# Two transformer blocks on one core: queue entries set behind their producers, staging by head groups, another opening order, and three PSUM banks for the last stage

## The reference

```
for layer in (0, 1):
    h = layernorm(x) * n1_g + n1_b
    x = attention(h, h,   q1, k1, v1, o1) + x      # 512 keys
    h = layernorm(x) * n2_g + n2_b
    x = attention(h, ctx, q2, k2, v2, o2) + x      # 1601 keys
    h = layernorm(x) * n3_g + n3_b
    a, g = split(h @ ff_w1 + ff_b1)
    x = (a * gelu(g)) @ ff_w2 + ff_b2 + x          # exact gelu
```

## Time and profile before

| | |
|---|---|
| median of 3 runs | 3865.36 us (3864.6 to 3879.61) |
| the profiled execution | 3857.31 us |
| its span | 3855.5 us |
| busy: PE, DVE, ACT, POOL | 3224.7, 2090.1, 1996.1, 624.3 us |
| mean granted clock of PE | 0.914 of full speed |

### The profile page before, as it was taken

The page is one execution under the profiler, slowest core; times in us unless marked ns, Lnnn a source line. Parts: engine busy times, 40 slices in busy tenths (PEclk is TensorE's granted clock), DMA queues, the critical chain, the costliest instruction groups (busy, mean ns, idle before and its releaser), DMA issues.

```text
span 3855.5 us, 43782 instructions
## 1 busy us (share of the span) xinstructions
PE 3224.7 (84%) x16320; PEld 1495.8 (39%) x16320; DVE 2090.1 (54%) x2565; ACT 1996.1 (52%) x3816; POOL 624.3 (16%) x676
## 2 busy tenths in 40 slices
PE   3686788899789878989889887898989979887867
PEld 1233343334344433534345332444334534533334
DVE  2554565667546655567546655555756645455410
ACT  1353366556555555556554565555655556454521
POOL 2113121212202121021201132021210031001010
PEclk9798898889899988999889998999989989998979
DMA  2642335431433344332333445333333133222202
GB/s 72 159 133 60 81 87 139 113 92 43 120 94 86 81 96 114 78 104 65 109 92 78 114 111 144 94 92 84 87 100 82 44 84 103 59 40 51 65 17 68
DMA packets 194323, 340.88 MB, mean 88 GB/s; under 512 B 19192, under 2 KB 101504, under 8 KB 192832
## 3 DMA queue, kind: packets, MB, share of 16 engines
q1 hardware_dynamic: 194112, 338.08, 33.7%
HBM read 202.29 MB, written 114.75 MB: 82 GB/s over the span
## 4 chain that ended last, share of the span: by engine, by line
PE 62%; DMA 11%; DVE 9%; ACT 6%; SPq 5%; issue 4%; POOL 3%; ACTq 0%; DVEq 0%; POOLq 0%
PE po L1053 12%; PE pr L1038 12%; PE pd L1019 8%; DVE mx L854 7%; DMA QS<-scr_q 6%; PE pf L969 5%; PE pf L977 5%; PE pf L916 4%; PE pf L957 3%; PE pf L939 3%; PE pf L948 3%; ACT ET L779 3%; DMA scr_k<-HS 2%; SPq L513 2%; PE pf L972 2%
## 5 line engine op out<-in xcount | busy, mean ns | idle before, releaser
L779 ACT ACTIVATE ET<-pr 128x512 f32<-128x512 f32 (+1 forms) x2720 | 1478.4, 597 | 1418.5 <-PE pr L1038 1406.0
L854 DVE TENSOR_REDUCE mx<-pd 128x2 f32<-128x804 f32 (+2 forms) x1600 | 1582.7, 1032 | 1056.2 <-PE pd L1019 1052.7
L1038 PE MATMUL pr<-QS,KS 64*128 64x512 f32 (+1 forms) x2720 | 877.1, 514 | 80.4 <-ACT ET L779 77.9
L1019 PE MATMUL pd<-KS,QS 64*128 64x400 f32 (+2 forms) x3200 | 636.4, 396 | 308.3 <-DMA QS<-scr_q 200.8
L1053 PE MATMUL po<-ET,V 128*32 128x512 f32 (+2 forms) x5440 | 779.9, 648 | 0.8 <-issue 0.6
L1038 PEld LDWEIGHTS pr<-QS,KS 64*128 64x128 f32 (+1 forms) x2720 | 345.3, 188 | 948.4 <-ACT ET L779 638.1
L1019 PEld LDWEIGHTS pd<-KS,QS 64*128 64x128 f32 x3200 | 374.4, 200 | 422.8 <-DMA QS<-scr_q 213.5
L673 POOL TENSOR_TENSOR HS<-uT,HS 128x512 fp32r<-128x512 f32 (+2 forms) x168 | 190.0, 1131 | 737.6 <-ACT uT L744 737.6
L969 PE MATMUL pf<-HS,WS 128*128 128x512 f32 x800 | 241.1, 433 | 72.2 <-DVE uT L847 24.9
L689 POOL TENSOR_TENSOR OA<-OA,DEN 128x512 f32<-128x512 f32 (+1 forms) x48 | 60.9, 1269 | 1311.4 <-DVE DEN L862 1311.4
L862 DVE RECIPROCAL DEN<-DEN 128x128 f32<-128x128 f32 (+1 forms) x192 | 170.5, 922 | 104.4 <-DMA DEN<-OU 103.7
(11 more groups left out here) (63 smaller groups left out, 2174.7 us busy)
## 6 DMA issues: line engine op xcount, KB each, us to landing
WS<-parts SPq DMA_DIRECT2D x160, 320.0 KB, 2.9
KS<-scr_k SPq DMA_DIRECT2D x80, 600.8 KB, 10.3
QS<-scr_q SPq DMA_DIRECT2D x80, 512.0 KB, 10.6
scr_k<-HS SPq DMA_DIRECT2D x144, 200.0 KB
scr_q<-HS SPq DMA_DIRECT2D x96, 256.0 KB
KS<-scr_k SPq DMA_DIRECT2D x80, 192.0 KB, 3.6
scr_k<-HS SPq DMA_DIRECT2D x48, 256.0 KB
OA<-OU SPq DMA_DIRECT2D x320, 32.0 KB
```

Source lines behind the costliest of these rows:

```text
L779: activation(ET[0:q.rows[k], s % 2, 2 * pair + e, :], pr[e][0:q.rows[k], :], ACT.Exp).then_inc(score_free, 1)
L854: v.reduce_max(mx[:, t, 2 * p:2 * p + 2, c], pd[no % 2][:, :, 0:cols], AX_X).then_inc(unit_free, 1)
L1019: ins = mm(pd[no % 2][:, e, 0:cols], queries[:, t * P:(t + 1) * P], keys, start=True, stop=True)
L1038: mm(pr[e][0:m, :], keys, queries, start=True, stop=True).then_inc(score_ready, 1)
```

## The change

- **SP's order.** `beside` becomes three functions: loads are queued `LOAD` = 2 beats behind their fill, stores 4 (`STORE`), bias rows 8 (`LOAD_ROW`). `MOVE` goes from 6 to 8, `INVERT` from (13, 15, 17, 19) to (14, 15, 16, 17), `DIVIDE` from 20 to 18.
- **Staging.** `KEY_JOBS` puts all key columns of a block of eight heads together; `split_for(q)` names the last fill that a group needs, and only that is waited for. Units start at `_at + 7`.
- **Prologue.** Of q1 and k1 only the first fill of each stands before the first beat; the others go into phase (None, 0). In phase (None, 1) v2a and a part of k2 come first, the rest of k2 and of q1, k1 of pass 2 goes to phase (0, 2). The memsets of KS come after the first statistics. v1 of pass 1 is set step by step into the last steps of phase (None, 0).
- **Bias rows** are added to X after the fourth normalisation, not after each.
- **Fills.** `deal_by_steps` gives each step one fill, or two of the short ones (t1, t2, t3, tc); ff2 has two parts of ten matmuls (`half`, `ff2`) at two steps; a gate starts with 4 fills of a instead of 3; two fills of v2a stand before t3. This holds for phases with a self and a cross pass, without those that split ff_w1 for `deal_by_steps`.
- **Last stage.** From `TAIL` (o2 of pass 7) fills go round `pf`, `pr[0]`, `pr[1]`, each with its own semaphore; g of pass 7 is evicted by Gelu itself; X of a layer 1 pass is stored tile by tile.

```diff
@@ -50,11 +50,15 @@
 V2B_GROUP = 2
+KEY_JOBS = [(c, n, cols) for c in range(KC) for n, cols in CHUNKS]
...
@@ -74,7 +78,8 @@
 def gate(i, together):
-    return [("gelu", i, 0)] + places("a", i, 0, together), places("a", i, together) + places("ff2", i)
+    return [("gelu", i, 0)] + places("a", i, 0, together), (
+        places("a", i, together) + [p for f in range(TT) for p in (("half", i, f), ("ff2", i, f))])
@@ -84,17 +89,25 @@
 def stages_beside(c, i):
     if c is None and i == 0:
-        seq = (mixed(places("tc", 0), places("n1", 1)) + places("t1", 1) + places("q1", 1) + places("k1", 1)
-               + places("k2", 0))
+        seq = [p for f in range(1, KC) for p in (("q1", 0, f), ("k1", 0, f))]
+        seq += mixed(places("tc", 0, 0, 3), places("n1", 1)) + places("t1", 1)
+        seq += [p for f in range(KC) for p in (("q1", 1, f), ("k1", 1, f))]
+        seq += places("tc", 0, 3) + places("k2", 0, 0, len(CHUNKS))
     elif c is None:
-        seq = (places("v1", 1) + places("o1", 0) + mixed(places("v2a", 0), places("n2", 0)) + places("t2", 0)
-               + mixed(places("q2", 0), places("n1", 2)) + places("t1", 2) + places("q1", 2) + places("k1", 2))
+        at = len(CHUNKS)
+        seq = places("v2a", 0) + [p for f in range(TT) for p in (("o1", 0, f), ("n2", 0, f))]
+        seq += places("k2", 0, at, at + 2) + places("t2", 0) + places("q2", 0, 0, 1)
+        seq += mixed(places("k2", 0, at + 2, 2 * at), places("n1", 2)) + places("q2", 0, 1) + places("t1", 2)
+        seq += [("q1", 2, 0), ("k1", 2, 0)]
     elif c == N - 1:
         first, rest = gate(c - 1, 3)
         seq = places("v2b", c) + mixed(places("o2", c - 1), []) + places("n3", c - 1) + places("t3", c - 1)
         seq += places("g", c - 1) + [first] + rest
     else:
         seq = places("v1", i) if i is not None else places("v2b", c)
+        if c == 0:
+            seq += [("q1", 2, 1), ("k1", 2, 1)] + places("k2", 0, 2 * len(CHUNKS))
+            seq += [("q1", 2, 2), ("k1", 2, 2)]
         seq += (places("o2", c - 1) if c else []) + places("o1", c + 1)
         cross = places("tc", c + 1)
         if i is not None:
...
@@ -105,10 +118,11 @@
         seq += places("k2", c + 1)
         if c % B == 0:
             seq = mixed(seq, places("w", c // B))
+        behind = places("v2a", c + 1)
         if c:
-            first, rest = gate(c - 1, 3)
-            seq += places("t3", c - 1) + places("g", c - 1) + [first] + rest
-        behind = places("v2a", c + 1)
+            first, rest = gate(c - 1, 4)
+            seq += behind[:2] + places("t3", c - 1) + places("g", c - 1) + [first] + rest
+            behind = behind[2:]
         if c + 3 < N:
             behind = mixed(behind[:2], places("n1", c + 3)) + behind[2:]
             behind += places("t1", c + 3) + places("q1", c + 3) + places("k1", c + 3)
...
@@ -116,7 +130,7 @@
     return [p if isinstance(p, list) else [p] for p in seq]
-BEFORE = places("n1", 0) + places("t1", 0) + places("q1", 0) + places("k1", 0) + places("v1", 0)
...
@@ -175,6 +189,13 @@
+COPY, MOVE, INVERT, DIVIDE = 5, 8, (14, 15, 16, 17), 18
+LOAD, STORE, LOAD_ROW = 2, 4, 8
...
+SHORT = ("t1", "t2", "t3", "tc")
+def deal_by_steps(stretches, steps):
+    slots, kinds = [], []
+    for stretch in stretches:
+        works = [p[0] for p in stretch if p[0] in STAGE or p[0] == "half"]
+        if works and works[0] in SHORT and slots and kinds[-1] == works[0] and len(slots[-1]) == 1:
+            slots[-1].append(stretch)
+        elif slots and kinds[-1] is None:
+            slots[-1][-1] = slots[-1][-1] + stretch
+            kinds[-1] = works[0] if works else None
+        else:
+            slots.append([stretch])
+            kinds.append(works[0] if works else None)
+    assert len(slots) <= len(steps)
+    for k, slot in enumerate(slots):
+        for n, stretch in enumerate(slot):
+            PLACES.setdefault(4 * steps[k * len(steps) // len(slots)] + 1 + 2 * n, []).extend(stretch)
...
+        for _f in range(TT):
+            PLACES.setdefault(4 * (_from - TT + _f + 1) + 5, []).append(("v1", _i, _f))
+        _v2a = len(VALUE_FILLS["v2a"])
+        deal(_all[:_v2a], _odd[2:2 + 2 * _v2a])
+        _q2 = [("q2", 0, 0)]
+        _fast = _all.index(_q2) + 1
+        _behind = [b for b in _odd if b > 4 * _from + DIVIDE]
+        _fills = sum(p[0] in STAGE for s in _all[_v2a:_fast] for p in s)
+        deal(_all[_v2a:_fast], _behind[:_fills])
+        deal(_all[_fast:], _behind[_fills:])
+    elif _i is not None and _c % B:
+        deal_by_steps(_all, range(_from + 1, _to))
     else:
         deal(_all, _odd[2::2])
 PLACES[BEATS + BEATS_BEHIND] = list(BEHIND)
...
+TAIL = FILL["o2", N - 1, 0]
+def split_for(q):
+    own = [("q" if x == "q" else "k") + ("1" if q.kind == "S" else "2") for x in "qk"]
+    fills = [(own[0], q.i, q.g // 2)]
+    if q.kind == "S":
+        fills.append((own[1], q.i, q.g // 2))
+    else:
+        fills.append((own[1], q.i, len(CHUNKS) * (q.g // 2 + 1) - 1))
+    return max(fills, key=lambda p: SPLIT[p])
...
-    _at = max(4 * _host.end if _host else FIRST_BEAT, _stored + 1 if _stored >= 0 else FIRST_BEAT)
+    _at = max(4 * _host.end if _host else FIRST_BEAT, _stored + STORE + 1 if _stored >= 0 else FIRST_BEAT)
     STAGE_AT.setdefault(_at, []).append(_q)
     if _q.n == 0:
         TURN_AT[FIRST_BEAT] = _q
         continue
-    _from = max(_at + 5, _free, 0)
+    _from = max(_at + 7, _free, 0)
...
-    _free = _beats[-1] + _lag + 1
+    _free = _beats[-1] + _lag + 2
...
-COPY, MOVE, INVERT, DIVIDE = 5, 6, (13, 15, 17, 19), 20
...
+        def free(no):
+            return fill_free if no < TAIL else tail_free[(no - TAIL) % len(tail_free)]
+        def freed_through(no):
+            if no < TAIL:
+                return [(fill_free, no + 1)]
+            return [(free(m), (m - TAIL) // len(tail_free) + 1) for m in range(max(no - len(tail_free) + 1, TAIL), no + 1)]
+        def bank(no):
+            return pf if no < TAIL else (pf, pr[0], pr[1])[(no - TAIL) % len(tail_free)]
...
+            for p in BEFORE:
+                stores_behind(*p)
+                loads_behind(*p)
+            for p in BEFORE:
+                row_behind(*p)
+            for beat in range(FIRST_BEAT, BEATS + BEATS_BEHIND + LOAD_ROW + 1):
+                for p in PLACES.get(beat - LOAD, []) if beat - LOAD >= 0 else []:
+                    loads_behind(*p)
+                for p in PLACES.get(beat - STORE, []) if beat - STORE >= 0 else []:
+                    stores_behind(*p)
+                for p in PLACES.get(beat - LOAD_ROW, []) if beat - LOAD_ROW >= 0 else []:
+                    row_behind(*p)
                 for q in STAGE_AT.get(beat, []):
...
-                pool.wait_ge(w_in["b"], LOADED["b", stage, i])
-                pool.wait_ge(norm_done, at + 1)
-                gp.tensor_tensor(X[:, b, t, :], X[:, b, t, :], brow[:, :], ALU.add).then_inc(bias_done, 1)
+                if t == TT - 1:
+                    pool.wait_ge(w_in["b"], LOADED["b", stage, i])
+                    pool.wait_ge(norm_done, at + 1)
+                    for k in range(TT):
+                        gp.tensor_tensor(X[:, b, k, :], X[:, b, k, :], brow[:, :], ALU.add).then_inc(bias_done, 1)
...
+                    activation(uT[:, f * T:(f + 1) * T], pf[:, :], ACT.Gelu if i == N - 1 else ACT.Identity,
+                               bias=b1col[:, l, 1, f:f + 1]).then_inc(done, 1)
...
+            def set_key_rows():
...
+                    set_key_rows()
...
+                if stage == "half":
+                    pe.wait_ge(fill_free, FILL["ff2", i, f])
+                    feed_back(bank(FILL["ff2", i, f]), i, f, range(FM // 2))
...
+                no, pf = FILL[stage, i, f], bank(FILL[stage, i, f])
+                if 0 < no <= TAIL:
+                    pe.wait_ge(fill_free, no)
+                elif no >= TAIL + len(tail_free):
+                    pe.wait_ge(free(no), (no - TAIL) // len(tail_free))
...
-                    if q.g == 0:
-                        pe.wait_ge(fill_free, filled("v1" if q.kind == "S" else "v2a", q.i))
+                    if q.g == 0 and q.kind == "C":
...
+                if q.g == 0 and q.kind == "S":
+                    pe.wait_ge(fill_free, FILL["v1", q.i, k] + 1)
...
```

More of the change, by code:

```diff
@@ L184, in deal @@
 def deal(stretches, beats):
-    count = sum(any(p[0] in STAGE for p in stretch) for stretch in stretches)
+    count = sum(any(p[0] in STAGE or p[0] == "half" for p in stretch) for stretch in stretches)
     k = 0
@@ L198 @@
     elif _c is None:
-        deal(_all[:TT], list(range(4 * _from + 4, 4 * _from + 8)))
-        deal(_all[TT:], [b for b in _odd if b > 4 * _from + 22])
+        for _f in range(TT):
[10 more added lines that the diff above has]
+        deal_by_steps(_all, range(_from + 1, _to))
     else:
@@ L413, in blocks_kernel @@
         fill_free = sem("fill_free")
+        tail_free = [sem(f"tail_free{i}") for i in range(3)]
         low_done = sem("low_done")
```

(9 more changed lines are left out.)

146 lines of the change are left out of this document (78 added, 68 removed).

## The result

The kernel after the change takes 3717.33 us (median of 4 runs, 3704.01 to 3730.65), the kernel before 3864.98 (4 runs). The ratio is 0.961, with a 95% interval of 0.9568 to 0.9652: 3.9% less time, where 6.7% was forecast (3608 us). The direction came as forecast and the two ends gave at least what was forecast; the middle gave back little more than a quarter of what was forecast there, and the time is by number that of case B (3718). The profiled execution took 3730.65 us, its span is 3728.8, its granted clock 0.925.

The account below looks back on a forecast made before the run. PE was taken to bound the middle, with its idle and lower-clock time to win. From the 3857.3 us execution, -50+11-9-150-70-12+40-17 = -257 gave 3600, so 3608 us for the median; range 3480 to 3765.

Parts of the forecast that it names:

- case B: Half of the middle's gain, waits moving to chunks, ACT holds for HS or DMA bandwidth: 3718 us (3690-3760), chance 0.22.
- Prologue, -50: Before the first unit: memsets 31.4 us, bias additions 2.6 and four projections 16.1 leave the path, together -50 us.
- the wait of 9.2 us in phase (None, 0): PE's wait at 132.9 for DVE, behind second-sequence statistics, goes as four projections come ahead: -9 us (0 to -9).
- contention at nothing: Prologue: DVE memsets beside POOL normalisations stop nothing, 0 us; a full block would be +31.
- Last stage, -17: Tail, 3711 us to the end: fills of g and save 10, hand-overs 4, bias additions 3, together -17 us.
- Staging, -150: PE's waits for QS in units: 110 us saved at 512 keys and 40 at 402 keys, through SP's order and later units.
- The clock, -70: Middle: fewer QS waits win back lower-clock time, 70 us of the 165 taken as lost; bounds 20 and 130.
- VectorE at 258 ... of 433 us has room.: Inner phase 836 to 1269: DVE busy 258 of 433 us, so PE bounds the middle and DVE has room.
- New waits, +40, less 12 for t3: Middle: late ff_w1 chunks and ACT holds cost +40 us (0 to 120); ACT's wait for k2's stores before t3 gives -12.
- the ring's hold: HS's ring of three: 15 us round against 12 needed, no hold; ACT waits 2 us on some splits where ff_w1 is split.
- the signs that the prediction was to be wrong: WS waits or ACT's store holds past 100 us, POOL's normalisations stretching beside memsets, or QS wait above 120 us.
- those that were to bear it out: First unit near 54 us, staging at scores' end, QS 40-60 us, clock 0.95, no t3 wait, last stage about 128 us.

Follow-up runs that it names:

- half maxima: The changed kernel with each maximum reduced over only the first half of a unit's columns, all else kept: 3588.11 us, ratio 0.9301 to the kernel before.

## Why the prediction was right in direction and too large

**Prologue, -50: -51.1.** Each part held: memsets (33.8 us alone), the first unit at 52.5 where 53 to 54 were forecast, the wait of 9.2 us in phase (None, 0) gone (the longest wait for maxima is now 1.1), contention at nothing. The Trainium skill (SBUF — State Buffer, "Who interferes with whom") says that a DVE instruction with at most one SBUF input, outside the two-port modes, does not contend with GpSimd; the rows agree, 1.44 and 1.45 us for a normalisation beside a memset and 1.45 without.

**Last stage, -17: -24.7.** The pace is the chunk's, as forecast; the banks were priced at 14 and bring about 15 at a like clock. Stages with these banks and a clock like that of before took 126 to 128 us, which is -17 to -19; some 6 of the 24.7 us are a kinder clock in this execution, which is luck.

**Staging, -150: -102, and -41 that had no term.** SP's place in the order was the mechanism: without the delays 60 us are lost, without the two beats 42. Two sizes were off. SP was to be on time and is still 3.7 us late at group 25, behind one block of 7.32 us; and the two beats of later units take nothing from the 11.9 us that the data need. The 41.0 us "issue" of the earlier trace rows were shown and not priced: the wait for the copy of the maxima went with the later units and `_free`, in the kernel before too (41.7 to 0).

**The clock, -70: some -8 by the estimate above. This is the step that failed.** It stood as "A saved wait also saves clock". I had taken the time at the lower clock as a consequence of long waits, by QS's share of the idle time. The sum itself was off too: three quarters of 193 us and the 12 of the other wait, of 497, make some 52 of the 165 us, not 70. But 430 us of PE's work are still done there, and 241 of them in 42 of the 70 stretches that hold no wait of PE over 3 us. Some of it lies where PE takes turns with VectorE, as in this piece of the kernel after, all at granted clock 0.50:

```profile
313.50 0.70 PE L1135 MATMUL pd<-KS,QS 64*128 64x400 f32 x2 [0.76 <-DVE mx L960]
314.39 0.70 PE L1135 MATMUL pd<-KS,QS 64*128 64x400 f32 x2 [0.20 <-DVE mx L960]
...
316.19 0.70 PE L1135 MATMUL pd<-KS,QS 64*128 64x400 f32 x2 [0.20 <-DVE mx L960]
317.09 0.70 PE L1135 MATMUL pd<-KS,QS 64*128 64x400 f32 x2 [0.20 <-DVE mx L960]
```

A unit each 0.9 us (two matmuls), released by a maximum. The row counts 0.70 of 0.90 us as busy, so by busy share this looks like PE's stage; by its pace it is VectorE's. The same turns a few us earlier, at the upper level:

```profile
304.00:306.00 2.00, 1.32 (x8) 0.80 (x8) 2.00 (x4) 0.00 (x0) 0.00 (x0) 1.00 0.00 0
...
305.13 0.46 PE L1135 MATMUL pd<-KS,QS 64*128 64x400 f32 x2 [0.45 <-DVE mx L960]
```

There PE needs 0.46 us and waits 0.45: again 0.9 us a unit. So for the units in such turns the lower level costs no time, and the upper would give none back. The end of long waits took hardly any work out of the lower level (432 to 430; 426 with hardly any wait for QS left). The Trainium skill (TensorE: Matmul & The Clock Gate, "A second HAM failure mode: psum-queue depth-cycling") tells of a kernel that idles briefly between groups of matmuls as it goes round its banks, and whose clock swings between the levels. This trace has such short waits (0.20 us) at the lower level; that they hold the clock there no run here shows, for the half maxima took them away and the averages fell by 28 us only. What holds most of the 430 us at the lower level stays open.

**"VectorE at 258 ... of 433 us has room."** The same error at its root: a mean over a phase. In a group's units, the two buffers of `pd` and 1033 ns for the reduction of one of them set the pace. So when staging no longer kept units apart, they met the maxima: 87 pieces more of that wait, 13 us by the list, 22 without the old piece of 9.2. Another 60 us stand in the units' busy time (631 against 571 with half maxima; 636 in the kernel before), where I had taken them for PE's work. Units later by four beats and nothing else cost 75 us; units later in the old kernel gave 18 of the 109 us that they saved at the data and at the copy. The time of case B, 3718, was met by luck: its middle was to give 80 us and gave 51, the ends gave 9 more than forecast, and its causes, chunks, holds and DMA bandwidth, were not the main ones.

**New waits, +40, less 12 for t3.** The wait that stood before t3's overwrite of HS is gone, as forecast, and the ring's hold came where it was forecast only for ff_w1: at k2 in phase (4, 6), where a fill of k2 stands in each step and the splits of ff_w1 go through the same ring (17.6 to 30.0 us, 11 of the 12 in this phase; with earlier stores it is 16.6 us shorter). Fills of g and a cost 9 us in the middle, k2 12; what else makes up the 42 us are scores (8) and small pieces. Of the signs that the prediction was to be wrong, WS or holds past 100 us or QS above 120, none came; of those that were to bear it out, three did not come either: QS at 40 to 60 us (98), staging at the end of the host's scores (3.7 us late), a clock of 0.95 in the middle (0.93).

**The middle as a sum.** Forecast -190: -159 for staging and X, -70 clock, +28 new waits less t3, +11 for the moved projections. Measured -51: -129 idle before units, +42 other idle time, +36 busy time, of which 11 are the projections. The 139 us between are 30 at the units (48 at QS and 22 at the maxima, less the 41 of the copy), some 70 at the clock, 14 at other waits and 25 of busy time that no step had. These 25 do not stand in the hand-over: the units' row counts 636 us before and 631 after. Fills of g and a rise most, from 334 to 352 us, and 160 of their 1120 matmuls start at the lower level in place of 84; why the lower level falls there now, no run here shows.

## What to carry to other kernels

Price a hand-over between two engines by its pace, unit by unit over its banks, not by the busy share of a phase: an engine at 60% can be the bound for each stretch in which its work comes. Let a queue entry stand behind the end of its producer and not beside its start, since everything behind it on that queue waits along; and look for the place where late data and crowded consumers cost the same, because past it each beat of delay costs more than it saves. Don't count clock as won back with each saved wait: here the time at the lower level fell by 117 us, and about 100 of them were the waits themselves. And compare the clock of several executions before a change is said to have moved it.

## What the runs showed of the hardware

The lower clock was held through stretches that the profile counts as mostly busy. Two of them, kernel after, columns as in the stretches above:

```profile
310.00:316.00 6.00, 5.03 (x22) 1.91 (x14) 4.07 (x5) 1.53 (x3) 0.00 (x0) 0.50 0.00 0
316.00:322.00 6.00, 5.42 (x20) 2.10 (x22) 3.73 (x5) 1.41 (x3) 0.00 (x0) 0.50 0.00 0
```

PE at 5.03 and 5.42 of 6 us, clock 0.50 in both, with no DMA and no wait longer than 0.8 us in the piece shown. The time at the lower level differed by up to 67 us between executions of one kernel (480 to 547 us with half maxima). And the busy time of the same 3200 matmuls moved by 60 us with the length of another engine's instruction, so a difference of a few per cent in PE's busy time is not by itself a difference in its work.
